# The last tile's expert logits of the lower mixture layer: half of them, and their sum, moved inside the loop over the steps

## The reference

```python
def kmoe(x_flat, W_router, A, B, scale, bias, d_in1, d_in2, d_out1, d_out2, top_k):
    logits = x_flat @ W_router.T                 # 64 experts
    vals, idx = jax.lax.top_k(logits, top_k)     # top 2
    probs = jax.nn.softmax(vals, axis=-1)
    xs = x_flat.reshape(-1, d_in1, d_in2)
    Ag = A[idx]
    Bg = B[idx]
    Y = jnp.einsum('nkoi,nij,nkpj->nkop', Ag, xs, Bg)
    out = jnp.einsum('nkop,nk->nop', Y, probs).reshape(-1, d_out1 * d_out2)
    return out * scale + bias
h = kmoe(x_flat, W_up, A_up, B_up, ..., 32, 32, 64, 64, 2)
h = jax.nn.gelu(h, approximate=False)
y = kmoe(h, W_down, A_down, B_down, ..., 64, 64, 32, 32, 2)
```

## Time and profile before

| | us |
|---|---|
| median of 3 runs | 1375.26 (1373.11 to 1378.72) |
| the profiled execution | 1373.84 |
| its span | 1372.0 |
| TensorE busy | 1262.5 (92%) |
| VectorE busy | 799.0 (58%) |
| ScalarE busy | 444.6 (32%) |
| GpSimd busy | 227.8 (17%) |
| share of TensorE in the chain that ended last | 76% |

### The profile page before, as it was taken

The page is one execution under the profiler, slowest core; times in us unless marked ns, Lnnn a source line. Parts: engine busy times, 40 slices in busy tenths (PEclk is TensorE's granted clock), DMA queues, the critical chain, the costliest instruction groups (busy, mean ns, idle before and its releaser), DMA issues.

```text
span 1372.0 us, 61950 instructions
## 1 busy us (share of the span) xinstructions
PE 1262.5 (92%) x27944; PEld 817.2 (60%) x27944; DVE 799.0 (58%) x1495; ACT 444.6 (32%) x927; POOL 227.8 (17%) x372
## 2 busy tenths in 40 slices
PE   6999999999999999999999997977888888898886
PEld 4865333333333334676666675666777777787775
DVE  2264776776777671556556553637273845357766
ACT  0222131122122112222122221336363636246554
POOL 0000000000000001222122220225152433113212
PEclk9999999999999999999999998989999999669998
DMA  6677889989989973411100111003330306513102
GB/s 257 217 243 198 283 292 306 308 276 318 300 279 319 292 282 88 77 61 61 61 31 31 61 46 62 32 2 153 92 123 31 122 0 246 213 66 128 82 36 92
DMA packets 68080, 211.50 MB, mean 154 GB/s; under 512 B 14448, under 2 KB 30832, under 8 KB 53520
## 3 DMA queue, kind: packets, MB, share of 16 engines
q1 hardware_dynamic: 67984, 210.16, 45.5%
HBM read 172.37 MB, written 37.75 MB: 153 GB/s over the span
## 4 chain that ended last, share of the span: by engine, by line
PE 76%; DVE 9%; issue 5%; DMA 4%; POOL 2%; SPq 1%; ACT 1%; DVEq 0%; POOLq 0%; ACTq 0%
PE ps L686 14%; PE ps L537 10%; PE ps L1058 8%; PE ps L2104 5%; DVE arena L549 4%; PE ps L234 4%; PE ps L1172 4%; PE ps L1079 4%; PE ps L2058 4%; PE ps L2073 3%; PE ps L444 3%; PE ps L2090 2%; PE ps L676 2%; PE ps L2037 2%; PE ps L2147 2%
## 5 line engine op out<-in xcount | busy, mean ns | idle before, releaser
L549 DVE STREAM_TRANSPOSE arena<-arena 128x448 f32<-128x448 f32 (+1 forms) x512 | 263.4, 577 | 100.1 <-PE ps L537 81.9
L537 PE MATMUL ps<-arena 32*64 32x400 f32 (+1 forms) x4096 | 202.5, 506 | 0.8
L686 PE MATMUL ps<-arena 128*64 128x512 f32 x832 | 189.2, 598 | 0.0
L537 PEld LDWEIGHTS ps<-arena 32*64 32x64 f32 x4096 | 75.0, 130 | 97.5 <-issue 50.2
L686 PEld LDWEIGHTS ps<-arena 128*64 128x64 f32 x832 | 55.6, 136 | 121.3 <-issue 111.9
L570 ACT ACTIVATE arena<-ps,arena 128x384 f32<-128x384 f32 x64 | 36.3, 582 | 276.4 <-DVE arena L561 276.4
L1971 ACT COPY arena<-ps 128x512 f32<-128x512 f32 x128 | 75.1, 587 | 144.2 <-PE ps L2073 81.1
L1058 PE MATMUL ps<-arena 128*128 128x256 f32 x512 | 115.3, 383 | 0.8 <-ACT arena L993 0.8
L1058 PEld LDWEIGHTS ps<-arena 128*128 128x128 f32 x512 | 97.3, 192 | 17.5 <-issue 3.3
L1800 DVE SCALAR_TENSOR_TENSOR arena<-ps,arena 128x512 f32<-128x512 f32 x64 | 68.9, 1104 | 37.7 <-PE ps L2090 37.5
L2104 PE MATMUL ps<-arena 64*64 64x32 f32 x4096 | 84.7, 236 | 6.3 <-DVE arena L1817 5.7
(11 more groups left out here) (144 smaller groups left out, 1859.5 us busy)
## 6 DMA issues: line engine op xcount, KB each, us to landing
arena<-ctx SPq DMA_DIRECT2D x64, 1024.0 KB
arena<-ctx SPq DMA_DIRECT2D x32, 768.0 KB
arena<-q_n SPq DMA_DIRECT2D x64, 256.0 KB, 11.3
h_n<-arena SPq DMA_DIRECT2D x16, 1024.0 KB, 4.5
arena<-h_n SPq DMA_DIRECT2D x16, 1024.0 KB, 9.5
arena<-x SPq DMA_DIRECT2D x16, 512.0 KB, 4.4
arena<-ctx SPq DMA_DIRECT2D x32, 256.0 KB
x_n<-arena SPq DMA_DIRECT2D x16, 512.0 KB, 3.5
```

The source lines that it names most:

```text
L537: last = pe.matmul(ps[b * SEQ:(b + 1) * SEQ, tb, 0:WIDTH[tb]], qs[p % 2][r, db, b * SEQ:(b + 1) * SEQ], z[r, at % RING, b, 0:WIDTH[tb]], s ...
L549: vec.transpose(z[:, at % RING, :, g * 224:g * 224 + nt * 32].rearrange("p b (j t) -> p b j t", t=32), slots[slot_of(k)][:, :, 0:nt, db * ...
L686: last = pe.matmul(ps[b * SEQ:(b + 1) * SEQ, OB, :], probt[:, j, b * SEQ:(b + 1) * SEQ], slot[:, b, jj, :], start=j == 0, stop=j == TILES - 1)
```

## The change

The 128 logits instructions of the last tile are cut in two. The first 64 stay where they were. The other 64 go into the loop over the steps, under `If(i < 1)`, between the two steps of the first trip. The fold goes to the head of the loop, under `If(i > 0)` and `If(i < 2)`, so that it is executed in the second trip. TensorE's wait for `s_lge` goes. On VectorE the two copies go from ahead of the steps into the steps n = 1 and n = 2 of tile 0.

```diff
             for n in range(STEPS):
                 if n + 2 < STEPS:
                     stage_h(T, n + 2)
+                if T == 0 and n == 1:
+                    parts(T_N, 6)
+                if T == 0 and n == 2:
+                    logits(vec, "dn", T_N - 1, 6)
                 y_out(T, n)
...
-        def logits_dn(bank):
-            for p in range(F1):
+        def logits_dn(bank, part=range(F1)):
+            for p in part:
...
-            last.then_inc(s_lgd, 1)
+            if p == F1 - 1:
+                last.then_inc(s_lgd, 1)
...
             with pe.Fori(T * 8, T * 8 + 7) as i:
+                with pe.If(i > 0):
+                    with pe.If(i < 2):
+                        fold_dn(T_N, 6)
                 second_dn(i * 2, 0)
                 first_dn(i * 2 + 2, 0)
+                with pe.If(i < 1):
+                    logits_dn(6, range(F1 // 2, F1))
                 second_dn(i * 2 + 1, 1)
                 first_dn(i * 2 + 3, 1)
...
-        logits_dn(6)
-        fold_dn(T_N, 6)
-        pe.wait_ge(s_lge, 9)
+        logits_dn(6, range(F1 // 2))
         with pe.Fori(0, T_N) as T:
             steps_dn(T)
```

More of the change, by code:

```diff
@@ L1918, in _ @@
                         stage_h(T, 1)
-            if T == 0:
-                parts(T_N, 6)
-                logits(vec, "dn", T_N - 1, 6)
             for n in range(STEPS):
```

## The result

The changed kernel took 1388.01 us in the median of six runs (1382.36 to 1398.23) where the kernel before took 1373.81 (six runs, 1373.11 to 1378.72); the ratio is 1.0081, with a 95% interval of 1.0043 to 1.012. Run once more on another chip beside further kernels it took 1391.5 against 1375.5, a ratio of 1.0109 (1.006 to 1.0158). The forecast was 1371 in a range of 1362 to 1382.

A forecast was written before the change was run, and what follows sets the result against it. TensorE was taken as the bound, with tile 0's steps slowed by a clock fallen behind the hand-over's idle times. Terms -2.0 - 1.1 - 13.0 + 12.2 = -3.9 us gave 1369.9, a median of about 1371, range 1362 to 1382.

The forecast's parts named there:

- (d): Three added branches in each of 28 trips: 0.5 us a trip, 3.5 in tile 0, 8.7 in tiles 1-3, loss 12.2 us.
- (c): Clock stays at 1.00 in tile 0: its steps gain 10.1 us, the stretch behind them 2.9, together 13.0 us.
- rival 4: Clock falls in a later tile, each trip idling 0.5 us more: one tile 1379 us, two or more 1386 and over; chance 0.08.
- What bounds the kernel: TensorE has 76% of the chain; behind the hand-over's idle times the clock falls, costing more than the idle time itself.
- (a): Fold's gap at the hand-over from logits to steps: both waits covered, the four fold matmuls stay at about 0.4; gain 2.0 us.
- (b): TensorE's 3.12 us stop for code near the first trip: two boundaries at 2.0 us together instead; gain 1.1 us.
- Rival 5: The code, one packet longer, no longer fits and each tile fetches all again: +21 us, 1392 us; chance 0.05.
- rivals 2 and 4: Rival 2: dear branches, over 0.7 us a trip, at 0.85 +5.2 us, 1380 us, chance 0.10; rival 4 has its own line.
- Rival 3: Clock falls in tile 0 all the same and stays down to the gather: +5.6 us, 1381 us; chance 0.15.

The follow-up runs named there:

- late_loads: Kernel before, with SyncE's loads behind the logits held back until four second products of tile 0 are done; ratio 1.0 (0.9969 to 1.0031).
- head_fold: Changed kernel with all logits ahead of the loop, the fold still at the head of the second trip under two branches; two runs, 1367.2 and 1399.7 us.
- mid_half: Changed kernel with nothing at the head; second half of logits and fold in the first trip's middle under one branch; 1365.8 us in two runs, ratio 0.99.
- mid_fold: Changed kernel with all logits ahead of the loop, nothing at the head, fold in the first trip's middle under one branch; 1381.96 us, ratio 1.0001.
- after_again: The changed kernel itself run again, unaltered, beside the kernel before; 1391.5 us, ratio 1.0109.
- mid_half_again: The mid_half kernel in more runs, against the kernel before; 1368.82 us in the median of 11, ratio 0.9951.
- head_two: Kernel before with two nested branches meant for the head of each trip; only one unconditional jump was built; ratio 0.9988.
- mid_long: Kernel before with a branch meant to jump 64 logits instructions mid-trip; an unconditional jump to the next instruction was built; ratio 1.0003.
- mid_short: Kernel before with a branch meant to jump two fold instructions mid-trip; an unconditional jump to the next instruction was built; ratio 1.0008.
- mid_half_late: mid_half with the loads behind the logits held back until four second products of tile 0 are done; 1374.13 us, ratio 0.9972.
- tile0_apart: mid_half with tile 0 written out apart, so the branch stands only in its trips and tiles 1 to 3 loop without it; 1370.72 us, ratio 0.9955.
- peeled: Changed kernel without its branches, tile 0's first trip written out ahead of the loop, its other trips written out too; 1387.51 us, ratio 1.005.

## Why the prediction was wrong, step by step

Two steps failed. **(d)** set the price of the branches too low, 8.7 us for tiles 1 to 3 where some 14 were measured. And **(c)** was worked out for tile 0 alone: the sum has no term for the clock in tiles 1 to 3, which was left to rival 4 at 0.08, and there it fell in both profiles. The second is the larger. With the measured price and the clock held, my sum would have come to about 1376 us (1371 + 5.3), still within the range. That the clock would hold in the later tiles rested on its holding there before, in spite of gaps of 0.90 and 0.53 us, while each of their trips was given more idle time.

**What bounds the kernel** was right. So was the reading of tile 0, in the main: the clock fell there behind the fold's waits and stayed down for the steps, and with them gone it held in both profiles of the changed kernel. late_loads shows that the waits are enough without the stop behind them; head_fold, which has neither those waits nor the changed kernel's second half of the logits in the loop, lost the clock in tile 0 all the same. So the step from waits that are gone to a clock that holds was not safe, and that it held was in part luck. One reading of mine was wrong: the clock was not at 1.00 all the way up to 1182. It had been at 0.50 from 1170.0 to 1172.5, behind a wait of 1.77 us for the staging of h, and came back within the logits (0.98 from 1172.5 to 1182.0).

**(a)**, the fold's gap, was right in kind: both waits are gone and 0.29 us of idle time is left. But the fold takes 0.65 us where I had 0.4, so the gain was some 1.5 us and not 2.0. **(b)** was right in kind: the stop of 3.12 us became one of 0.52 in this profile and two of 0.80 and 0.44 in the second, where I took 2.0 for two. late_loads shows the cause, since the stop shrank to 0.50 us when nothing but the loads was moved. **(c)** held for tile 0: (a), (b), (c) and tile 0's share of (d) were to make the stretch from the logits to the transposes 9.7 us shorter (2.0 + 1.1 + 10.1 - 3.5), and it was 9.1; the stretch behind it gave 1.4 instead of 2.9. The 29 us that I named for tile 0's steps left out the half of the logits and the fold that now stand in them; they took 35.4.

**(d)** in detail. The price was set at 0.5 us a trip, and the trips of tile 0 show 0.97: 0.49 at the head where I had 0.3, and 0.49 in the middle where I had 0.2. Alone they cost 0.47 (head_fold) and 0.34 (mid_half, mid_fold), and together more than their sum. That is not paid in full in every trip, since waits for VectorE hide some of it. The steps of tile 3, at the full clock in the second profile of the changed kernel (after_again) and in mid_half:

```profile
1347.00:1378.00 31.00, 23.42 (x1408) 21.06 (x1408) 17.38 (x30) 15.52 (x29) 8.94 (x15) 1.00 0.17 68
1326.40:1355.00 28.60, 23.28 (x1408) 20.95 (x1408) 17.02 (x30) 15.53 (x29) 9.17 (x15) 1.00 0.19 73
```

Before they took 26.3. So three branches cost 4.7 us in this tile and one costs 2.3, where I had 2.9 for three; for the three tiles that is 14.0 instead of 8.7. My upper bound of 1.03 a trip held it, but I chose by a row of 0.29 that stands at another place of the program, behind a short product. The row of the branch back, 0.35 visible though it follows the longest product of the trip, was the nearer one. What hides a branch I could have read at the lower clock: a branch back is hidden there wholly, which suggests that TensorE has a backlog then, of which the full clock leaves little. That there is less of it for a second and third branch is argued from this, not shown by a run of its own.

**Rival 4**, the clock falling in a later tile, had 0.08 and is what happened. Its mechanism, idle time added to every trip, fits the falls within the steps: tiles 2 and 3 in the first profile, the last trips of tile 2 in the second. It did not name the entry of tile 1, where the clock fell in both, and where the head's branches lengthen a wait that was there. Nor is a trip 4.92 us at the lower clock, as it had: it takes 5.41 (1241.22 to 1246.63), with 0.43 of idle time at the head. From the traces, idle time in us around tile 1's entry and what the clock did there:

| kernel | stop for code | before the first second product | clock at the entry |
|---|---|---|---|
| before | 0.44 | 0.42 | holds |
| mid_half | 0.72 | 0.42 | holds |
| mid_half_again | 0.44 | 0.41 | holds (falls two trips on) |
| changed | 0.73 | 1.05 | falls |
| after_again | 0.44 | 1.05 | falls |
| head_fold | 0.44 | 0.91 | falls |
| mid_fold | 0.99 | 0.42 | falls |
| head_two | 1.00 | 0.50 | falls |

late_loads, mid_long, mid_short and mid_half_late have at most 0.71 and 0.42 there and hold too; tile0_apart has 0.62 and 0.39, and falls behind the stop of 1.45 that follows. In these traces the falls at tile 1's entry are those with 0.91 us or more in one of the two places or just behind. This is a list of cases and no measure for other places. At the entries of tiles 2 and 3 some 1.00 us stands ahead of the first second product before and after the change, with no stop for code near it, and the clock held at all of them. In tile 0 it held in mid_half behind 1.40 and 0.52 us, with logits between them, and fell in head_fold behind 0.40 and 0.79. What decides it stays open.

Once down, it stays for the tile; the changed kernel's profile has 38.9 us for tile 1's steps. Of the 33.0 us that tiles 1 to 3 lost there, 14.0 are the branches' by the price of tile 3 above, so some 19 are the clock's (an estimate, since tile 3 stands for all three; 21 trips at 0.97, the most that the branches can take, would leave 12.6). Against my sum that profile is 28.3 us over: 19 for the clock, 5.3 for the price in tiles 1 to 3, 0.6 in tile 0, 1.5 behind it, and 1.9 for the late start. I had set rivals 2 and 4 beside each other as alternatives. The range should have held their sum, 1380 and 7.5 to 15 more, so up to 1395. That idle time from branches also makes a fall likelier is argued: for it, nine of eleven runs of mid_half hold the clock and no run of the changed kernel reaches their 0.979; against it, mid_fold.

**Rival 5** fell: between 1240 and 1396 no packet of queue 8 shows in the changed kernel, so the code of a tile, one packet longer, is still kept; this is the view of its queues there, with no line for queue 8.

```profile
q14 instruction: 3, 0.02, 0.1%
```

Between 1174 and 1240 queue 8 brought eight packets. The Trainium skill ("Runtime: NRT & Kernel Launch", Instruction fetch mechanics) gives TensorE 128 KiB, filled in blocks of 16, from which an estimate of eight blocks follows; the trace agrees with that. On the Trainium skill's rule on jumps in the same section, my ground was too thin: the branch back over more than one packet can stay within two blocks. The loop over T is what disagrees with the rule, since it jumps back over a whole tile's code and no packet comes.

The Trainium skill ("Advanced Engine Details and Errata", Control Flow Timing) states about 108 ns for a compare-and-branch, which makes an estimate of 0.32 us for three. The trace doesn't agree: it shows up to 0.97, of which 0.15 is the slower second product in the middle.

**Rival 3** did not come true in either profile of the changed kernel: tile 0 stayed at 1.00.

mid_half gives a rough check of the account. It has the gain of tile 0 and one branch a trip, and in its first profile its clock held in all four tiles. Its missing pair at the head is worth 2.4 us in tile 3, so some 9.6 in four tiles, and with that its 1366.9 to 1369.8 become 1376 to 1379. The best run of the changed kernel took 1382.36, at a mean clock of 0.977 where those have 0.979 to 0.984, so a piece of a tile at the lower clock may be the rest; no profile shows that run.

## What to carry to other kernels

A branch inside a hardware loop is paid in each trip of each tile, however seldom its body runs: multiply it by all trips first, and take its price from the branch back in the same loop, not from one at another place of the program. To take the branches away by writing the code out can cost as much, when that code has to be fetched while short matmuls run. Where a stage doesn't win back the clock by itself, give its fall a term of its own in every such stage, not only in the one that the change touches, and look for idle time that the change adds at its entry or in its trips; here that was worth more than the instructions moved.

## What the runs showed of the hardware

- A comparison that jumps costs the same over two matmul instructions (mid_fold) as over 66 (mid_half): 3.77 us a trip in both. An unconditional jump in the same place cost 0.04 at most.
- In many trips the 32 matmuls right after a comparison in the middle came slower, 0.52 to 0.61 us instead of 0.46 with three comparisons in the trip, and 0.49 to 0.63 with one. So part of the price of a branch stands in the rows as busy time of TensorE and not as idle time.
- Stops for code with no data packets beside them took 0.42 to 1.67 us in these traces (mid_long, mid_half_late). With the loads at 92% or more of the engines they took 2.51 to 4.92 (peeled, mid_short), and 0.79 in head_fold with the loads at 77%.
- The steps of the lower layer keep the full clock in most tiles but did not regain it in any trace: in tile 0 of the kernel before it came back only in the next gather, some 44 us later. At the lower clock the pair at the head was still in sight, 0.43 us of idle time a trip in tile 1 of the changed kernel, while the branch back alone was not.
